# A top-25 neighbour gather: the scores of the gathered tile are made by ScalarE and GpSimd instead of VectorE, its indices and bounds by GpSimd

## The reference

```python
mask = A != 0
scores = jnp.where(mask, -jnp.arange(N), -jnp.inf)
vals, idx = jax.lax.top_k(scores, 25)
feats = jax.vmap(lambda x, i: x[i])(X, idx)          # absent neighbours count as -inf
agg = feats.max(axis=2)
agg = jnp.where((mask.sum(-1) <= 25)[..., None], jnp.maximum(agg, 0.0), agg)
out = jax.nn.relu(jnp.concatenate([X, agg], -1) @ W + b)
return _layernorm(x + out)
```

## Time and profile before

| | us |
|---|---|
| median of 3 runs | 584.74 (583.03 to 585.98) |
| profiled execution, its own time | 587.01 |
| its span, first to last instruction | 585.3 |
| VectorE (DVE) busy | 530.7 (91%) |
| TensorE (PE) busy | 509.4 (87%) |
| ScalarE (ACT) busy | 400.4 (68%) |
| GpSimd (POOL) busy | 289.2 (49%) |

### The profile page before, as it was taken

One profiled execution on the slowest core, in us unless ns is written; L12 is line 12 of the kernel. 1 busy time (PEld: TensorE's weight loads), 2 busy tenths in 40 slices (PEclk: granted clock), 3 DMA queues, 4 the chain that ended last, 5 costly groups with the idle time before them and its releaser, 6 DMA issues.

```text
span 585.3 us, 13962 instructions
## 1 busy us (share of the span) xinstructions
PE 509.4 (87%) x4600; PEld 346.0 (59%) x4600; DVE 530.7 (91%) x977; ACT 400.4 (68%) x761; POOL 289.2 (49%) x462
## 2 busy tenths in 40 slices
PE   3687998899969998899988999799988999779982
PEld 2444675567645675566755576556755667546761
DVE  5976999999998999999998988999999999998894
ACT  6832667468974788658965788568886589546744
POOL 3633573357434774247533565237742475337700
PEclk9587999999999999999988999799999999999997
DMA  7753544466655645565535645267565653021102
GB/s 259 188 160 83 138 126 102 123 137 134 97 112 146 168 111 124 136 155 125 136 93 148 141 130 111 78 171 170 110 120 140 157 123 61 2 60 44 47 8 73
DMA packets 84418, 69.48 MB, mean 119 GB/s; under 512 B 56259, under 2 KB 72902, under 8 KB 84294
## 3 DMA queue, kind: packets, MB, share of 16 engines
q1 hardware_dynamic: 77894, 54.93, 38.9%
q0 software_dynamic: 6400, 13.12, 8.5%
HBM read 50.99 MB, written 4.19 MB: 94 GB/s over the span
## 4 chain that ended last, share of the span: by engine, by line
PE 38%; DVE 34%; issue 12%; DVEq 7%; ACT 4%; DMA 3%; POOL 0%; POOLq 0%; SPq 0%; ACTq 0%
PE pair L1074 30%; DVE part L801 15%; DVE hot L796 5%; DVE g_feat L874 4%; DVEq L871 2%; DVE g_val L842 2%; PE misc L1119 2%; DVE agg_t L901 2%; DVEq L940 2%; PE p_V L1057 1%; DMA adj_sb<-in_adj 1%; PE misc L1120 1%; DVE g_score L844 1%; DVEq L1008 1%; DVEq L917 1%
## 5 line engine op out<-in xcount | busy, mean ns | idle before, releaser
L1074 PE MATMUL pair<-hot,x_part 128*128 128x128 bf16 (+3 forms) x3120 | 411.9, 280 | 32.9 <-DVE part L801 28.2
L1074 PEld LDWEIGHTS pair<-hot,x_part 128*128 128x128 bf16 x3120 | 239.0, 99 | 141.5 <-issue 46.3
L801 DVE TENSOR_REDUCE part<-pair 128x128 f32<-128x1024 f32 (+1 forms) x256 | 279.3, 1100 | 25.5 <-PE pair L1074 24.0
L485 POOL DMA_INDIRECT g_feat<-in_x,g_idx x200 | 193.7, 968 | 127.0 <-issue 81.3
L605 ACT ACTIVATE V<-p_V 128x512 bf16<-128x512 f32 x98 | 57.7, 588 | 68.9 <-PE p_V L1057 68.9
L532 POOL TENSOR_TENSOR y_sb<-relu_sb,x_sb 128x128 f32<-128x128 f32 x64 | 30.6, 479 | 149.1 <-ACT relu_sb L659 148.5
L633 ACT ACTIVATE hot<-V,first_bias 128x1024 bf16<-128x1024 bf16 x56 | 64.0, 1142 | 25.6 <-PE pair L1074 25.6
L796 DVE TENSOR_SCALAR hot<-V 128x1024 bf16<-128x1024 bf16 x224 | 79.4, 375 | 0.0
L648 ACT ACTIVATE hot<-distance,one 128x1024 bf16<-128x1024 bf16 x56 | 63.9, 1141 | 0.2
L641 ACT ACTIVATE distance<-V,second_bias 128x1024 bf16<-128x1024 bf16 x56 | 63.6, 1136 | 0.0
L598 ACT ACTIVATE mask<-adj_sb 128x1024 bf16<-128x1024 uint32 x56 | 58.7, 1049 | 6.5 <-DMA adj_sb<-in_adj 6.5
(11 more groups left out here) (92 smaller groups left out, 431.9 us busy)
## 6 DMA issues: line engine op xcount, KB each, us to landing
adj_sb<-in_adj SPq DMA_DIRECT2D x56, 512.0 KB
g_adj<-in_adj SPq DMA_DIRECT2D x8, 512.0 KB, 4.4
x_sb<-in_x SPq DMA_DIRECT2D x8, 512.0 KB, 4.6
out<-y_sb SPq DMA_DIRECT2D x7, 512.0 KB, 5.2
g_feat<-in_x,g_idx POOLq DMA_INDIRECT x200
maskT<-mask SPq DMA_TRANSPOSE x49
out<-y_sb SPq DMA_DIRECT2D x1, 448.0 KB
w_sb<-in_W SPq DMA_DIRECT2D x1, 128.0 KB, 6.2
```

The lines of the kernel that those rows point to most:

```text
L485: pool.indirect_dma_start(out=g_feat[w][:, k, :], out_offset=None, in_=x_rows, in_offset=bass.IndirectOffsetOnAxis(ap=g_idx[w][:, k:k + 1] ...
L801: dve.tensor_reduce(part[:, par(q, s), :, p], slots_of(q, s, p).rearrange("f k i -> f i k"), AX.X, ALU.max).then_inc(s_used, 1)
L1074: last = pe.matmul(dst, x_part[:, q, part_no, kb], one_hot, start=(first and part_no == 0), stop=(final and part_no == PARTS - 1))
```

## The change

The scores of tile 0 for batches 2 to 8 are no longer made by VectorE. ScalarE writes the sign of the adjacency row into `g_score` as the last thing of its first step (`find0`), and GpSimd multiplies it in place by `falling` at the start of its step 2 (`score0`). The small operations behind the search go to GpSimd, at the end of its step 7 (`index0`). The search itself stays on VectorE, and its steps 1 and 2 come later: step 1 behind group 4 of step 2 instead of group 1, step 2 behind group 1 of step 3 instead of group 4 of step 2. The first batch's search stays on VectorE as it was.

```diff
+SEARCH = LAST_STEP - 1
...
                     if s == 1 and not last:
-                        sp.wait_ge(s_ex, LAST_STEP * (2 * i + q) + 1)
+                        if is_first(i, q):
+                            sp.wait_ge(s_score, 1)
+                        else:
+                            sp.wait_ge(s_found, 2 * i + q)
                         load_adj0(ni, nq)
...
+            def score0(batch):
+                wait(s_found, batch)
+                pool.tensor_tensor(g_score[0][:, :], g_score[0][:, :], falling[:, :], ALU.mult).then_inc(s_score, 1)
+
+            def index0(batch, bp):
+                val, pick, step = g_val[0], g_pick[0], 3 * (batch - 1)
+                wait(s_ex, SEARCH * (batch + 1))
+                pool.tensor_scalar(first0[:, :], val[:, 0:1], 0.0, val[:, 0:1], ALU.is_equal, ALU.add).then_inc(s_index, 1)
+                pool.wait_ge(s_index, step + 1)
+                pool.tensor_scalar(pick[:, :], val[:, 0:K], 0.0, first0[:, :], ALU.is_equal, ALU.mult).then_inc(s_index, 1)
+                pool.tensor_scalar(g_bound[0][:, bp, 0:1], val[:, K:K + 1], 0.0, -BIG, ALU.is_gt, ALU.mult
+                                   ).then_inc(s_bound, 1)
+                pool.tensor_scalar(g_bound[0][:, bp, 1:2], val[:, 0:1], 0.0, None, ALU.is_gt).then_inc(s_bound, 1)
+                pool.wait_ge(s_index, step + 2)
+                pool.tensor_tensor(pick[:, :], pick[:, :], val[:, 0:K], ALU.add).then_inc(s_index, 1)
+                pool.wait_ge(s_index, step + 3)
+                pool.tensor_scalar(g_idx[0][:, :], pick[:, :], -1.0, row_base[:, batch:batch + 1], ALU.mult, ALU.add
+                                   ).then_inc(s_idx0, 1)
...
                 for s in range(1, NT):
+                    if s == 2 and not last:
+                        score0(2 * i + q + 1)
                     if s <= 5:
                         gather0(i, q, s)
...
                     redo(i, q, s)
+                    if s == MT and not last:
+                        index0(2 * i + q + 1, nq)
...
+            def find0(batch):
+                act.wait_ge(s_adj0, 16 * (batch + 1))
+                act.wait_ge(s_ex, SEARCH * batch)
+                nc.scalar.activation(g_score[0][:, :], g_adj[0][:, :].bitcast(U32), ACT.Sign).then_inc(s_found, 1)
...
                     if to_rank:
                         copy_V(*to_rank, 1)
+                    if s == 1 and not last:
+                        find0(2 * i + q + 1)
...
-                if st > 0:
-                    dve.wait_ge(s_ex, LAST_STEP * batch + st)
+                if st == 1:
+                    dve.wait_ge(s_score, batch + 1)
+                elif st > 1:
+                    dve.wait_ge(s_ex, SEARCH * batch + st - 1)
...
-            EXTRACT = {1: {4: 0}, 2: {1: 1, 4: 2}, 3: {3: 3}, 4: {3: 4}, 5: {1: 5, 3: 6}, 6: {}, 7: {1: 7, 3: 8}}
+            EXTRACT = {1: {}, 2: {4: 1}, 3: {1: 2, 3: 3}, 4: {3: 4}, 5: {1: 5, 3: 6}, 6: {}, 7: {1: 7}}
...
                         if (s, p) in GATHERED:
+                            if (s, p) == (7, 0) and not begin:
+                                dve.wait_ge(s_bound, 2 * (2 * i + q))
```

More of the change, by code:

```diff
@@ L194, in build @@
         g_bound = [sb(f"g_bound{w}", [P, 2, 2], F32) for w in range(2)]
+        first0 = sb("first0", [P, 1], F32)
         g_idx = [sb(f"g_idx{w}", [P, K], I32) for w in range(2)]
@@ L268, in build @@
         s_ex = sem("extraction0_step")
+        s_score = sem("scores0_ready")
+        s_index = sem("index0_step")
+        s_bound = sem("bounds0_ready")
+        s_found = sem("neighbours0_marked")
         s_adj0 = sem("adj0_loaded")
@@ L864, in extraction @@
                     if w == 0:
-                        ins.then_inc(s_ex, 1)
+                        ins.then_inc(s_ex if st > 0 else s_score, 1)
             def gathered_max(w, bp, signal, steps):
@@ L979, in step @@
                         if p in steps:
-                            if steps[p] == 0:
-                                dve.wait_ge(s_ex, LAST_STEP * (2 * i + q + 1))
-                                dve.wait_ge(s_adj0, 16 * (2 * i + q + 2))
                             extraction(0, 2 * i + q + 1, (steps[p],), nq, False)
```

## The result

The changed kernel takes 592.65 us (median of 6 runs, 590.64 to 593.85); the kernel before takes 585.55 us in the same comparison (median of 6, 583.03 to 588.83). The recorded ratio is 1.0104, with a 95% interval of 1.0078 to 1.0129 (the quotient of the two medians, 1.0121, lies inside it). The forecast was 586.3 us, at most 591.0, with a chance of 0.34 for slower. Where executions of one kernel fall into a shorter and a longer state, as those of e12 do, only the shorter ones are compared.

The account below looks back on a forecast made before the run. TensorE was taken to set the pace in steps 2 to 5, VectorE in 6, 7 and 1. Terms -5.1 + 1.4 + 2.0 + 2.3 + 1.0 = +1.6 us on the 584.74 median gave 586.3 us, range 581 to 591.

Parts of the forecast that it names:

- The product and the one-hots: Step 2: product and VectorE's one-hots hold each other up, 0.15 us a batch with the first one-hot ahead; +1.0 us.
- rival (B): Step 2: product starts first, the one-hot waits it out, VectorE 0.7 us later in 7 batches; 588.3 us, chance 0.13.
- The gathers: Step 6: product delays the last indirect loads, VectorE's first maximum waits; +2.0 us in five batches, +2.3 in batch 5.
- The index: Batch boundaries: index operations leave VectorE, 1.22 us gained at four of seven plus 0.2 for small things; -5.1 us.
- The order: Steps 2 and 3: later search steps 1 and 2 make VectorE about 0.2 us late in each of 7 batches; +1.4 us.
- The score operation: Start of step 2: seven score operations leave VectorE where TensorE sets the pace; costed at 0, 8.0 us if uncovered.
- The price of the product: GpSimd's step 2: an elementwise product of 1024 columns takes 2.5 us, between 1.23 and 3.12.
- The sign on ScalarE: End of ScalarE's step 1: the sign falls into 4.88 us of idle time; hidden, 0.

Follow-up runs that it names:

- e12: The changed kernel with the product moved into GpSimd's idle time of step 1; 596.63, 607.69, 608.13 and 608.74 us, where before takes 586.64.
- e4: The kernel before plus one 128x1024 product per batch on GpSimd at its step 2, into a tile nobody reads; 595.13 us, ratio 1.0152 to before.
- e14: The changed kernel with the eight subtractions in four pairs ahead of indirect loads of step 5; 589.53 us, ratio 1.0057 to before.
- e10: The changed kernel with the product in four pieces of 256 columns, one ahead of each of step 2's first four loads; 596.63 us, ratio 1.0178 to before.
- e16: The changed kernel with the product in four pieces of 256 columns and the eight subtractions in four pairs; 586.23 us, ratio 1.0012 to before.
- e1: The kernel before with only the index operations moved to GpSimd, scores and search as before; 582.66 us, ratio 0.994 to before.
- e3: The kernel before with only search steps 1 and 2 at their later places; 586.71 us, ratio 1.0005 to before.
- e11: The kernel before with VectorE's score operation cut to 8 columns in batches 2 to 8 (leaves work out); 584.66 us, ratio 0.9963 to before.
- e9: The changed kernel with the GpSimd product on 8 columns instead of 1024 (leaves work out); 589.4 us, ratio 1.004 to before.
- e13: The kernel before with the index on GpSimd and the later search steps, scores still on VectorE; 582.96 us, ratio 0.9935 to before.
- e15: The changed kernel with search steps 1 and 2 behind groups 2 and 4 of step 2; 594.17 us, ratio 1.0121 to before.
- e8: The kernel before with VectorE's score operation of batches 2 to 8 cut to 8 columns, on the chip where before takes 689.05 us; ratio 0.9981.

## Why the prediction was wrong

**The step that failed** is "The product and the one-hots", costed at +1.0 us with the one-hot of 190.67 ahead of the product. The forecast had the two starts 0.03 us apart (190.67 and about 190.7), read from two engines, and the race went the other way: in batches 2 to 7 the product was first five times, by 0.03 to 0.36 us, and the one-hot took 2.28 to 2.61 us. In batch 3 the one-hot was first by 0.03 us, and the next one took 1.45, as the forecast had it for that case. That is the mechanism of rival (B), which had 0.13 and was priced too low, with 0.7 us a batch. e4 has the product alone, so it covers this term and that of the gathers, +1.0 and +4.3 in the forecast; it measured +8.9, and its only wait for a load is as long as that of the kernel before (1.58 us). So nearly all of it falls on the one-hots, 1.3 us a batch.

A second reason no rival had: once GpSimd came late to step 4, its wait ahead of the residual (1.2 to 1.7 us before, batch 5 apart) was down to 0.01 us in batches 2 to 7, so loads, residual and eight subtractions ran on in one row, and this row held a one-hot of VectorE in three batches. In e4, whose shorter product leaves 0.36 us of that wait, it happened once, in batch 5, which had no such wait before the change either. Taking the row apart gives 2.8 us back in the changed kernel (e14), and 9.7 us where the product is in pieces (e10 to e16). The rule of the Trainium skill (SBUF — State Buffer, "Who interferes with whom") says that a VectorE instruction in a two-port mode and a GpSimd instruction exclude each other for the whole instruction; the runs agree for the single product, and they add that a row of instructions can hold VectorE nearly to its end.

**The gathers** were costed at +4.3 us (2.0 and 2.3) and this was wrong too. In the changed kernel VectorE waited for a load once, 0.26 us, in batch 5. GpSimd's last indirect load of that batch and VectorE's first maximum:

```profile
360.50 0.94 POOL L494 DMA_INDIRECT g_feat<-in_x,g_idx  x1 [0.30 <-issue]
363.04 1.76 DVE L918 TENSOR_TENSOR g_feat<-g_feat 128x1536 f32<-128x1536 f32 x1 [0.26 <-DMA g_feat<-in_x,g_idx]
```

The maximum starts 2.54 us after the load, so the forecast's bounds for the landing (up to 5.14, read from one wait in the same batch) were no constant: where a wait for the loads ended it, this distance was 2.51 to 6.34 us over all the kernels on chips where before takes about 586 us. In four of the seven batches (1, 2, 4 and 7) the distance is still the 5.03 us of before: the wait ahead of the residual took up the product, or VectorE came as late as the loads did. Two errors had opposite signs here, the gathers too dear and the one-hots too cheap, and without that luck the forecast would have been further off.

**The index** was right in place and mechanism: the four boundaries lose 0.95 to 1.21 us in step 7 of batches 1, 3, 5 and 7, 5.0 in sum over all, for 5.1 forecast; by the medians e1 gives 3.6.

**The order** was costed at +1.4 and measured +0.3 (e3), within its interval the same as nothing.

**The score operation** was costed at 0; e11 puts its full removal at 2 us. TensorE sets the pace behind it nearly, not wholly. This error made the result better than forecast, not worse.

**The price of the product** was 2.5 us; 2.36 was measured. The sign on ScalarE is hidden as forecast: ScalarE is busy 6.9 us longer (407.3 for 400.4), and behind the sign in batch 3 it still waits 4.04 us for TensorE (4.88).

What stays open: e9 and e13 differ by 1% although e9's product is short. Their traces put most of it on the hold and the late loads of batch 5 and the late loads of batch 3, but why the loads came late there was not traced. Nor was it settled why the eight subtractions hold a one-hot nearly to their end in some batches and let it through with 0.15 to 0.3 us more in others. The trace of before has only the latter, and e15, with one such hold, is no faster than the change with three.

## What to carry to other kernels

Before work goes to GpSimd because it has idle time, look at which VectorE instructions will run beside it. Here a long two-input GpSimd operation held a one-hot of VectorE for what was left of its length, and one unused product per batch cost 1.5% (e4); if it must go there, put it in short pieces with other things between (e16, with the row of subtractions taken apart too: 5.4 us back; pieces alone, e10, made it worse). A change that makes GpSimd late can also join operations of its own that used to be separated by a wait, so look for rows of them downstream. And take apart a change that bundles a gain and a loss: the index part alone is 0.6% faster than before.

## What was not expected of the hardware

- A row of eight GpSimd operations of 0.43 us held a VectorE one-hot of 0.18 us for 2.84 us, through the residual and seven of the eight, without letting it in between (step 4 of batch 3; in six batches of e10).
- The same product of 1024 columns took 2.36 us in place with two different tiles as operands and 1.89 with the same tile twice and another output (e4); 256 columns took 0.74 us (e16).
- Beside a product a reduction of VectorE kept its length (1.22 us at 189.85), while the one-hots did not.
- One of the four chips of the experiments ran the kernel before at 689.05 us instead of about 586; in e8's trace there, VectorE waits up to 6.2 us at a time for something that the profile doesn't name.
